# Layer 1's FFN: another order of TensorE's and VectorE's work within a round

## The chip, the cores and the metric

One NeuronCore of a Trainium2 chip runs the whole kernel as one program. The metric is the time of one execution on the device in microseconds (us), as the median of several runs.

## The reference

Two transformer layers on 1024 tokens (4 x 256) of width 512, each an attention and an FFN with a layer norm behind each of the four. The change touches only the last of the four, layer 1's FFN:

```python
result = jnp.einsum('bsi,oi->bso', x, W) + b                  # "base": 512 -> 512
q = jnp.einsum('bsi,ni->bsn', x, Wq).reshape(Bt, S, E, DK)    # E = 8 experts, DK = 32
k = jnp.einsum('bsi,ni->bsn', x, Wk).reshape(Bt, S, E, DK)
scores = jnp.einsum('bsed,bsed->bse', q, k) / math.sqrt(DK)
w = jax.nn.softmax(scores, axis=-1)                           # "gate"
h = jnp.einsum('bsi,eri->bser', x, A)                         # rank R = 16 each
combined = jnp.einsum('bse,bser,eor->bso', w, h, Bm)
x = _layernorm(x + result + combined)                         # the layer norm at the end
```

(The program prints `x + _L1_ffn_ref(x)`; the residual is folded into the rows that are added at the end of a tile.)

## The kernel before

The 1024 tokens are 8 tiles of 128 (`NT` = 8). Class `FFN1` (L2406) gives each engine its own program; each goes through rounds t = 0 to 8 (`rounds`, L2443): rounds 0 and 1 are written out, rounds 2 to 5 are a loop of two iterations with two rounds each, rounds 6, 7 and 8 are written out again. Every operand is kept as a high and a low part, so every product is three matmuls (`matmul3`: lines 106, 107, 108 are its three).

What TensorE does in a round t from 1 to 5, in its order (`round_` in `tensor`, L2730 on): `queries(t)`, 12 matmuls of 320 columns into bank `bq` (q and half of h); `turn_weighted(t - 1)`, one transpose of the weighted rows `wh` of the tile before into `bw`; `keys`, 12 matmuls of 320 columns into `bk` (k and the other half of h); `combined(t - 1)`, 3 matmuls of 512 columns that finish the sum of the tile before in `br`; `turn(t + 1)`, 4 transposes of the next tile's tokens `x` into `bx`; `base(t)`, 12 matmuls of 512 columns into `br`. `queries(t)` first waits for `xT_lo` of tile t, `turn(t + 1)` for `x` of tile t + 1, `turn_weighted` for `wh`, `combined` for `whT_lo`. Round 6 puts `queries(7)` and `keys(7)` after half of `base(6)`; round 7 holds `turn_weighted(6)`, the rest of `base(6)`, `combined(6)` and three quarters of `base(7)`; round 8 the rest.

VectorE in round t (`round_` in `vector`, L2659 on): `begin(t + 1)` writes `x` of the next tile (L2527); in rounds 0 and 1 statistics of later tiles of the norm before; `whT_lo` (L2669); then `gates_and_end` (L2603). That one mixes two chains. The gate of tile t: `gate_product` (L2544, waits for `bk`), `gate_scores` (L2548), `gate_max` (L2553), `gate_scaled_max` (L2557), after ScalarE's exponential `gate_weights` (L2562 to L2570, writes `wh`). The end of tile t - 1: `end_sum` (L2579, waits for `combined`), `end_stats` (L2584), `end_mean` (L2589), `end_var` (L2594), after GpSimd's power `end_out` (L2600, writes `yo`). Between them stands `xlo(t + 1)` (L2532, writes `xT_lo`, waits for ScalarE's `xT_hi`). A step that reads what VectorE has just written waits for it with a semaphore (`after`).

ScalarE in round t: `qs` (L2500), `whT_hi` (L2504), `xT_hi` of tile t + 1 (L2495), the exponential (L2509). GpSimd in round t (`round_` in `gpsimd`, L2475 on): `with_bias(t + 1)` (L2473, writes `xb`; it waits for `end_mean` of tile t - 1), in round 1 alone the power of four later tiles' variances of the norm before (`norm.power(pool, 4, 8)`, L1117), then the power of tile t - 1 (L2484, writes `rs`, for which `end_out` waits):

```python
if has(t + 1, NT):
    with_bias(t + 1, 1 - u)
if isinstance(t, int) and t == 1:
    norm.power(pool, 4, 8)
if has(t - 1, NT):
    ...
    pool.tensor_tensor(rstd[:, :], mean[:, 1:2], m["mh"][:, 0:1], ALU.pow).then_inc(s_rs, 1)
```

All queues run in program order; no planner sets it. SyncE only stores finished tiles.

Of the kernel before, what the change touches and what calls it, by code (L numbers as in the profile page):

```python
# [41 lines left out]
NT = T // P  # L42
KC = HID // P
# [24 lines left out]
def f32(ap):  # L68

    return ap.bitcast(F32)  # L70


def transpose(pe, out, rows, ident):

    return pe.transpose(out.bitcast(F32R), rows, ident)  # L75


def need(eng, sem, value):

    if isinstance(value, int) and value <= 0:  # L80
        return
    eng.wait_ge(sem, value)
# [16 lines left out]
def has(x, n):  # L99

    return not isinstance(x, int) or 0 <= x < n
# [2304 lines left out]
class FFN1:  # L2406
# [4 lines left out]
    def __init__(self, k, io, g, raw, norm):  # L2411
# [118 lines left out]
        def xlo(dve, t, u):  # L2530
            dve.wait_ge(s_xhi, t + 1)
            dve.tensor_tensor(xT[u][1][:, :], bx[:, :], f32(xT[u][0][:, :]), ALU.subtract).then_inc(s_xlo, 1)  # L2532

        def vector(dve, added):

            def after(sem, value):

                dve.wait_ge(sem, value)
                plain(dve, g["tick"])

            def gate_product(t, u):
                dve.wait_ge(s_q, t + 1)
                dve.wait_ge(s_bk, t + 1)
                dve.tensor_tensor(prod[:, :], bk[u][:, 0:E * DK], qs[:, :], ALU.mult).then_inc(s_gate, 1)  # L2544

            def gate_scores(t):
                after(s_gate, NGATE * t + 1)
                dve.tensor_reduce(sc[:, :], prod[:, :].rearrange("p (e d) -> p e d", e=E), AX, ALU.add)\  # L2548
                   .then_inc(s_gate, 1)

            def gate_max(t):
                after(s_gate, NGATE * t + 2)
                dve.tensor_reduce(nm[:, :], sc[:, :], AX, ALU.max, negate=True).then_inc(s_gate, 1)  # L2553

            def gate_scaled_max(t):
                after(s_gate, NGATE * t + 3)
                dve.tensor_scalar(nms[:, :], nm[:, :], inv, None, ALU.mult).then_inc(s_gate, 1)  # L2557

            def gate_weights(t, u):
                dve.wait_ge(s_ex, t + 1)  # L2560
                plain(dve, g["tick"])
                dve.reciprocal(ri[:, :], sm[:, :]).then_inc(s_gate, 1)  # L2562
                after(s_gate, NGATE * t + 5)
                dve.tensor_scalar(gate[:, :], ex[:, :], ri[:, 0:1], None, ALU.mult).then_inc(s_gate, 1)
                after(s_gate, NGATE * t + 6)
                need(dve, s_tw, t)
                for i, bank in enumerate((bq[u], bk[u])):
                    es = slice(i * E // 2, (i + 1) * E // 2)
                    h = bank[:, E * DK:W1H].rearrange("p (e r) -> p e r", e=E // 2)
                    dve.tensor_tensor(wh[:, es, :], h, gate[:, es][:, :, None].to_broadcast([P, E // 2, R]),  # L2570
                                      ALU.mult).then_inc(s_wh, 1)

            def end_tiles(t):
                return (y, st, mv, rs) if not isinstance(t, int) or t < NT - 1 else (x[0], st_last, mv_last, rs_last)

            def end_sum(t, v):
                dve.wait_ge(s_r, t + 1)
                dve.wait_ge(s_xb, t + 1)
                dve.tensor_tensor(end_tiles(t)[0][:, :], br[v][:, :], xb[v][:, :], ALU.add).then_inc(s_end, 1)  # L2579

            def end_stats(t):
                rows, stats, _, _ = end_tiles(t)
                after(s_end, NEND * t + 1)
                dve.bn_stats(stats[:, :], rows[:, :]).then_inc(s_end, 1)  # L2584

            def end_mean(t):
                _, stats, mean, _ = end_tiles(t)
                after(s_end, NEND * t + 2)
                dve.bn_aggr(mean[:, :], stats[:, :]).then_inc(s_end, 1)  # L2589

            def end_var(t):
                var = end_tiles(t)[2][:, 1:2]
                after(s_end, NEND * t + 3)
                dve.tensor_scalar(var, var, EPS, None, ALU.add).then_inc(s_var, 1)  # L2594
# [8 lines left out]
            def gates_and_end(t, u, before):  # L2603

                now, last = has(t, NT), has(t - 1, NT)
                early = isinstance(t, int) and t == NT - 2
                v = 1 - u
                if now:
                    gate_product(t, u)
                if last:  # L2610
                    end_sum(t - 1, v)
                if early:
                    xlo(dve, t + 1, v)
                if now:
                    gate_scores(t)
                if last:
                    end_stats(t - 1)
                if now:
                    gate_max(t)
                if last:  # L2620
                    end_mean(t - 1)
                if now:
                    gate_scaled_max(t)
                if last:
                    end_var(t - 1)
                if has(t + 1, NT) and not early:
                    xlo(dve, t + 1, v)
                if now:
                    gate_weights(t, u)
                if last:  # L2630
                    end_out(t - 1, v, before)
# [53 lines left out]
        def turn(pe, t, u):  # L2685
            pe.wait_ge(s_x, t + 1)
            need(pe, s_xlo, t)
            for c in range(KC):
                i = transpose(pe, bx[:, c * P:(c + 1) * P], x_t[u][:, c * P:(c + 1) * P], ident[:, :])
            i.then_inc(s_tx, 1)  # L2690
# [6 lines left out]
        def tensor(pe):  # L2697

            def queries(t, u):
                pe.wait_ge(s_xlo, t + 1)  # L2700
                need(pe, s_wh, 2 * t - 2)
                wide(pe, bq[u], u, HID, W1H, True).then_inc(s_bq, 1)

            def keys(u):
                wide(pe, bk[u], u, HID + W1H, W1H, True).then_inc(s_bk, 1)

            def turn_weighted(t):
                pe.wait_ge(s_wh, 2 * t + 2)
                need(pe, s_whl, t)
                transpose(pe, bw[:, 0:P], wh_t[:, :, :].rearrange("p e r -> p (e r)"), ident[:, :]).then_inc(s_tw, 1)  # L2710

            def combined_last():
                out, hi, lo = br[1][:, :], whT[0][:, :], whT[1][:, :]
                pe.wait_ge(s_whT, NT)
                pe.matmul(out, hi, bm[0], start=False, stop=False, skip_group_check=True)
                pe.matmul(out, hi, bm[1], start=False, stop=False, skip_group_check=True)
                pe.wait_ge(s_whl, NT)
                pe.matmul(out, lo, bm[0], start=False, stop=True, skip_group_check=True).then_inc(s_r, 1)

            def combined(t, v):  # L2720
                pe.wait_ge(s_whl, t + 1)
                if isinstance(t, int) and t == 0:
                    pe.wait_ge(raw["s_lo"], KC + 1)
                matmul3(pe, br[v][:, :], (whT[0][:, :], whT[1][:, :]), bm, False, True).then_inc(s_r, 1)

            def base(t, u, chunks=range(KC)):
                need(pe, s_end, NEND * (t - 2) + 1)
                wide(pe, br[u], u, 0, HID, False, chunks)

            def round_(t, u, i):  # L2730
                if isinstance(t, int) and t == NT - 1:
                    turn_weighted(t - 1)
                    base(t - 1, 1 - u, range(2, KC))
                    combined(t - 1, 1 - u)
                    base(t, u, range(KC - 1))
                    return
                if isinstance(t, int) and t == NT:
                    turn_weighted(t - 1)
                    base(t - 1, 1, range(KC - 1, KC))
                    combined_last()  # L2740
                    return
                if not (isinstance(t, int) and t == 0):
                    queries(t, u)
                    turn_weighted(t - 1)
                keys(u)
                if has(t - 1, NT):
                    combined(t - 1, 1 - u)
                turn(pe, t + 1, 1 - u)
                if isinstance(t, int) and t == NT - 2:
                    base(t, u, range(2))  # L2750
                    queries(t + 1, 1 - u)
                    keys(1 - u)
                else:
                    base(t, u)

            rounds(pe, round_)

        self.begin, self.xlo, self.turn, self.first = begin, xlo, turn, first
# [77 lines left out]
```

## Time and profile before

| | |
|---|---|
| time, median of 3 runs | 1416.83 us (1416.5 to 1417.45) |
| the profiled execution | 1415.87 us, its span 1414.1 us |
| mean granted TensorE clock | 0.999 |
| TensorE busy | 1400.2 us (99% of the span) |
| VectorE, ScalarE, GpSimd busy | 72%, 63%, 55% |
| stage of layer 1's FFN | from about 1347 us to the end |

Times in the rows are us from the start of the span. A matmul's recorded duration is longer than its step: matmuls are pipelined, so the distance from one start to the next is what one costs.

### The profile page before, as it was taken

What the parts mean: (1) busy time and instruction counts of PE and PEld (TensorE: products, weight loads), DVE (VectorE), ACT (ScalarE), POOL (GpSimd) and SP (SyncE); (2) the same over time, 40 slices, a digit from 0 to 9 for tenths busy, and PEclk for the clock granted to TensorE, in tenths of its full rate; (3) what the DMA queues carried; (4) which work ended last, traced back from release to release, by engine and by line L of the source; (5) the groups of instructions that cost most, each with busy time, mean ns of one, the idle gap of its engine ahead of it and who ended that gap; (6) DMA issues with size and microseconds to landing.
All of it is one profiled execution on the core that took longest, in us unless ns stands there. A gap on an engine that the chain in (4) does not pass through costs nothing.

```text
span 1414.1 us, 30207 instructions
## 1 busy us (share of the span) xinstructions
PE 1400.2 (99%) x8769; PEld 1236.6 (87%) x8769; DVE 1017.3 (72%) x2528; ACT 891.2 (63%) x2445; POOL 774.0 (55%) x828
## 2 busy tenths in 40 slices
PE   9999999999999999999999999999999999999998
PEld 7898889888788878889889889889889889889887
DVE  5999999999968875665665665665665665665776
ACT  5888888888555576555556556556556556556711
POOL 3555555555040467765765765665665665665521
PEclk9999999999999999999999999999999999999999
DMA  5533333322445301111101011001002001000201
GB/s 197 169 95 95 95 95 95 94 66 51 134 135 164 97 31 61 31 31 59 30 30 59 30 30 59 30 30 59 30 30 59 30 30 59 30 30 30 83 16 46
DMA packets 56155, 92.60 MB, mean 65 GB/s; under 512 B 6064, under 2 KB 27312, under 8 KB 56112
## 3 DMA queue, kind: packets, MB, share of 16 engines
q1 hardware_dynamic: 55968, 91.93, 21.3%
q8 instruction: 23, 0.38, 0.1%
q14 instruction: 20, 0.16, 0.0%
q10 hardware_dynamic: 144, 0.13, 0.0%
HBM read 81.82 MB, written 2.10 MB: 59 GB/s over the span
## 4 chain that ended last, share of the span: by engine, by line
PE 94%; DVE 2%; ACT 1%; issue 1%; POOL 1%; DMA 1%; SPq 0%; POOLq 0%; DVEq 0%; ACTq 0%
PE c_bv L106 8%; PE c_bv L108 7%; PE c_bv L107 7%; PE c_bx L106 5%; PE h_bo L944 5%; PE c_bx L108 4%; PE c_bx L107 4%; PE c_by L106 4%; PE c_by L108 4%; PE c_by L107 4%; PE h_bo L1447 3%; PE a_acc L1447 3%; PE h_bt L75 3%; PE h_bs L106 2%; PE c_bt L75 2%; PE h_bs L108 2%
## 5 line engine op out<-in xcount | busy, mean ns | idle before, releaser
L618 POOL TENSOR_TENSOR h_pr<-h_pr,h_rinv 128x512 f32<-128x512 f32 x128 | 133.2, 1041 | 136.7 <-DVE h_rinv L769 134.3
L1778 POOL TENSOR_TENSOR c_qk<-g_y,c_qk 128x512 fp32r<-128x512 f32 x96 | 124.0, 1292 | 147.3 <-ACT c_qk L1890 140.6
L1629 POOL TENSOR_TENSOR b_sw_lo<-b_slots,b_sw_hi 128x512 fp32r<-128x512 f32 (+1 forms) x128 | 148.1, 1157 | 10.2
L1627 POOL CAST b_sw_hi<-b_slots 128x512 fp32r<-128x512 f32 (+1 forms) x128 | 72.6, 567 | 143.6 <-DMA b_slots<-in_w_qk 125.5
L106 PE MATMUL c_bv<-b_wv_hi,g_xT_hi 128*128 128x256 f32 x496 | 138.8, 280 | 0.2 <-DVE g_xT_lo L1183 0.2
L108 PE MATMUL c_bv<-b_wv_hi,g_xT_lo 128*128 128x256 f32 x496 | 138.8, 280 | 0.0
L107 PE MATMUL c_bv<-b_wv_lo,g_xT_hi 128*128 128x256 f32 x496 | 138.7, 280 | 0.0
L1999 DVE TENSOR_TENSOR c_bo<-c_bo,g_wo 128x128 f32<-128x128 f32 x128 | 38.3, 300 | 122.3 <-ACT g_wo L1865 117.6
L1890 ACT ACTIVATE c_qk<-g_y 128x512 fp32r<-128x512 f32 x96 | 60.7, 632 | 96.5 <-DVE g_y L2036 67.1
L671 ACT ACTIVATE h_pr<-h_bs,h_nmax 128x256 f32<-128x256 f32 x256 | 119.3, 480 | 2.5 <-DVE h_nmax L764 2.4
L1855 ACT ACTIVATE c_pr<-c_pr,c_rinv 128x128 f32<-128x128 f32 (+1 forms) x256 | 101.8, 448 | 9.1 <-DVE c_rinv L1989 9.1
L1847 ACT ACTIVATE c_pr<-g_wo,c_nmax 128x128 f32<-128x128 f32 x128 | 51.5, 403 | 84.3 <-DVE c_nmax L1985 84.3
L107 PEld LDWEIGHTS c_bv<-b_wv_lo,g_xT_hi 128*128 128x128 f32 x496 | 93.1, 188 | 4.7
L106 PEld LDWEIGHTS c_bv<-b_wv_hi,g_xT_hi 128*128 128x128 f32 x496 | 93.0, 187 | 4.7 <-DVE g_xT_lo L1183 0.3
L1609 POOL TENSOR_TENSOR b_slots<-b_slots 128x256 f32<-128x256 f32 x128 | 93.8, 755 | 2.5
L108 PEld LDWEIGHTS c_bv<-b_wv_hi,g_xT_lo 128*128 128x128 f32 x496 | 93.1, 188 | 0.0
L2017 DVE TENSOR_TENSOR g_res<-c_bv,g_res 128x512 f32<-128x512 f32 x103 | 71.2, 692 | 27.2 <-PE c_bv L108 27.2
L764 DVE TENSOR_REDUCE h_nmax<-h_bs 128x2 f32<-128x512 f32 x128 | 87.5, 684 | 0.0
L773 DVE TENSOR_TENSOR h_pt_lo<-h_bt,h_pt_hi 128x512 fp32r<-128x512 f32 x128 | 87.2, 681 | 0.2
L1860 ACT ACTIVATE c_pt<-c_bt 128x384 fp32r<-128x384 f32 x128 | 62.9, 491 | 35.3 <-PE c_bt L75 31.5
L1865 ACT ACTIVATE g_wo<-c_bo 128x128 f32<-128x128 f32 x128 | 35.3, 276 | 77.3 <-PE c_bo L2262 77.3
L106 PE MATMUL c_bv<-b_wo_hi,c_oT 128*128 128x512 f32 x200 | 81.4, 407 | 0.0
(480 smaller groups left out, 5140.2 us busy)
## 6 DMA issues: line engine op xcount, KB each, us to landing
f_wi<-in_w_ffn SPq DMA_DIRECT2D x66, 256.0 KB, 2.7
b_slots<-in_w_qk SPq DMA_DIRECT2D x64, 256.0 KB, 3.0
a_w<-in_w_head SPq DMA_DIRECT2D x28, 352.0 KB, 2.9
h_part<-in_w_ffn SPq DMA_DIRECT2D x32, 264.0 KB, 2.7
b_raw_v<-in_w_v SPq DMA_DIRECT2D x16, 512.0 KB, 4.5
b_raw_o<-in_w_o SPq DMA_DIRECT2D x16, 512.0 KB, 4.5
h_o_mix<-h_o_hi SPq DMA_DIRECT2D x62, 128.0 KB, 2.2
b_ffn_w<-in_w_ffn SPq DMA_DIRECT2D x4, 576.0 KB, 5.6
```

Source lines behind the costliest of these rows:

```text
L106: pe.matmul(out, w[0], x[0], start=start, stop=False, skip_group_check=True)
L107: pe.matmul(out, w[0], x[1], start=False, stop=False, skip_group_check=True)
L108: return pe.matmul(out, w[1], x[0], start=False, stop=stop, skip_group_check=True)
L618: pool.tensor_tensor(pr[b][:, :, :], pr[b][:, :, :], rinv[b][:, :][:, :, None].to_broadcast([P, 2, S]), ALU.mult)\
L671: m = act.activation(pr[b][:, i, :], bs[b % 2][:, i * S:(i + 1) * S], ACT.Exp, bias=nmax[b][:, i:i + 1], accum_out=rsum[b][:, i:i + 1])
L764: dve.tensor_reduce(nmax[b][:, :], bs[b % 2][:, :].rearrange("p (a n) -> p a n", a=2), AX, ALU.max, negate=True).then_inc(s_max, 1)
L773: dve.tensor_tensor(pt[b][1][:, :, :], bt[b % 2][:, :].rearrange("p (a n) -> p a n", a=2), f32(pt[b][0][:, :, :]), ALU.subtract).then_inc( ...
L1447: m = pe.matmul(out, a, b, start=start and i == 0, stop=stop and i == len(pairs) - 1, skip_group_check=True)
L1609: pool.tensor_tensor(slot(out), slot(a), slot(b), op).then_inc(self.s_comb, 1)
L1629: pool.tensor_tensor(self.sw[1][:, a:b], self.slots[:, a:b], f32(self.sw[0][:, a:b]), ALU.subtract)\
L1778: pool.tensor_tensor(lo, src, f32(hi), ALU.subtract).then_inc(s_sumlo, 1)
L1855: m = act.activation(x[:, cols], x[:, cols], ACT.Identity, scale=rinv[t % 2][:, i:i + 1])
```

## The change

On TensorE, in rounds 1 to 6, `turn_weighted(t - 1)` moves from between `queries` and `keys` to behind `keys`, directly ahead of `turn(t + 1)`; `combined(t - 1)` moves from behind `keys` to behind the first half (two of four chunks) of `base(t)`; the second half of `base(t)` follows it. In round 6 `combined(5)` stands between the first half of `base(6)` and `queries(7)`. On VectorE, in all rounds but 7 and 8, the four steps of the gate follow one another, then comes `xlo(t + 1)`, and only then the four steps of the end of tile t - 1. ScalarE's, GpSimd's and SyncE's programs stay as they are.

```diff
                 if now:
                     gate_product(t, u)
-                if last:
-                    end_sum(t - 1, v)
                 if early:
                     xlo(dve, t + 1, v)
                 if now:
                     gate_scores(t)
-                if last:
-                    end_stats(t - 1)
-                if now:
                     gate_max(t)
-                if last:
-                    end_mean(t - 1)
-                if now:
                     gate_scaled_max(t)
-                if last:
-                    end_var(t - 1)
                 if has(t + 1, NT) and not early:
                     xlo(dve, t + 1, v)
+                if last:
+                    end_sum(t - 1, v)
+                    end_stats(t - 1)
+                    end_mean(t - 1)
+                    end_var(t - 1)
                 if now:
                     gate_weights(t, u)
...
                 if not (isinstance(t, int) and t == 0):
                     queries(t, u)
-                    turn_weighted(t - 1)
                 keys(u)
                 if has(t - 1, NT):
+                    turn_weighted(t - 1)
+                turn(pe, t + 1, 1 - u)
+                base(t, u, range(2))
+                if has(t - 1, NT):
                     combined(t - 1, 1 - u)
-                turn(pe, t + 1, 1 - u)
                 if isinstance(t, int) and t == NT - 2:
-                    base(t, u, range(2))
                     queries(t + 1, 1 - u)
                     keys(1 - u)
                 else:
-                    base(t, u)
+                    base(t, u, range(2, KC))
```

## Rows read from the trace of the kernel before

**Rows 1.** The page: busy time, share of the span and instructions of TensorE.
```profile
PE 1400.2 (99%) x8769; PEld 1236.6 (87%) x8769; DVE 1017.3 (72%) x2528; ACT 891.2 (63%) x2445; POOL 774.0 (55%) x828
```

**Rows 2.** Windows, the last stretch: five engines' busy us, granted clock, DMA share, GB/s.
```profile
1406.40:1414.10 7.70, 1.63 (x8) 1.02 (x6) 3.49 (x11) 1.09 (x2) 1.29 (x3) 0.80 0.21 72
```

**Rows 3.** Timeline of TensorE: start us, us, engine, line, operation; where queries follow.
```profile
1376.29 0.39 PE L108 MATMUL e_br<-b_ffn_hi,e_xT_lo 128*128 128x512 f32 x1
1376.75 0.41 PE L106 MATMUL e_bq<-b_ffn_hi,e_xT_hi 128*128 128x320 f32 x1
1377.00 0.31 PE L107 MATMUL e_bq<-b_ffn_lo,e_xT_hi 128*128 128x320 f32 x1
...
1398.47 0.41 PE L106 MATMUL e_bq<-b_ffn_hi,e_xT_hi 128*128 128x320 f32 x1
```

**Rows 4.** Timeline of TensorE in round 3: keys, combined, tokens turned, base.
```profile
1371.11 0.31 PE L107 MATMUL e_bk<-b_ffn_lo,e_xT_hi 128*128 128x320 f32 x1
...
1372.72 0.39 PE L106 MATMUL e_br<-b_ffn_hi,e_whT_hi 128*128 128x512 f32 x1
...
1373.41 0.45 PE L75 MATMUL e_bx<-g_ident,e_x_t 128*128 128x128 f32 x4
1373.70 0.47 PE L106 MATMUL e_br<-b_ffn_hi,e_xT_hi 128*128 128x512 f32 x1
1374.01 0.40 PE L107 MATMUL e_br<-b_ffn_lo,e_xT_hi 128*128 128x512 f32 x1
```

**Rows 5.** Timeline of VectorE in round 3.
```profile
1373.62 0.69 DVE L2579 TENSOR_TENSOR e_y<-e_br,e_xb 128x512 f32<-128x512 f32 x1 [0.20 <-PE e_br L108]
...
1375.38 0.18 DVE L2589 BATCH_NORM_AGGREGATE e_mv<-e_st 128x2 f32<-128x6 f32 x1
...
1375.93 0.69 DVE L2532 TENSOR_TENSOR e_xT_lo<-e_bx,e_xT_hi 128x512 fp32r<-128x512 f32 x1
```

**Rows 6.** Timeline of TensorE and ScalarE in round 1.
```profile
1353.75 0.30 PE L106 MATMUL e_bq<-b_ffn_hi,e_xT_hi 128*128 128x320 f32 x1
...
1355.99 0.27 ACT L2504 ACTIVATE e_whT_hi<-e_bw 128x128 fp32r<-128x128 f32 x1
```

**Rows 7.** Timeline of VectorE in round 0: the gate's chain with nothing between its steps.
```profile
1351.49 0.42 DVE L2548 TENSOR_REDUCE e_sc<-e_prod 128x8 f32<-128x256 f32 x1 [0.15 <-DVE e_prod L2544]
...
1352.45 0.68 DVE L2532 TENSOR_TENSOR e_xT_lo<-e_bx,e_xT_hi 128x512 fp32r<-128x512 f32 x1
```

**Rows 8.** Timeline of VectorE in round 8: the end's chain with nothing between its steps.
```profile
1408.07 0.69 DVE L2579 TENSOR_TENSOR e_x<-e_br,e_xb 128x512 f32<-128x512 f32 x1 [0.30 <-PE e_br L2718]
...
1409.74 0.18 DVE L2589 BATCH_NORM_AGGREGATE e_mv<-e_st 128x2 f32<-128x6 f32 x1
```

**Rows 9.** Timeline of GpSimd in rounds 1 and 3.
```profile
1360.37 1.29 POOL L2473 TENSOR_TENSOR e_xb<-e_x,b_ffn_b 128x512 f32<-128x512 f32 x1 [10.37 <-DVE e_mv L2589]
1361.62 1.02 POOL L1117 TENSOR_TENSOR g_rs<-g_mv,g_mh 128x4 f32<-128x4 f32 x1
1362.61 0.55 POOL L2484 TENSOR_TENSOR e_rs<-e_mv,g_mh 128x1 f32<-128x1 f32 x1
...
1375.64 1.28 POOL L2473 TENSOR_TENSOR e_xb<-e_x,b_ffn_b 128x512 f32<-128x512 f32 x1 [5.96 <-DVE e_mv L2589]
```

**Rows 10.** Timeline of VectorE from round 1 into 2, and in round 3.
```profile
1363.19 0.55 DVE L2600 TENSOR_SCALAR e_yo<-e_y,e_mv,e_rs 128x512 f32<-128x512 f32 x1 [1.00 <-POOL e_rs L2484]
1363.73 0.55 DVE L2527 TENSOR_SCALAR e_x<-g_res,g_mv,g_rs 128x512 f32 x1
...
1369.81 0.55 DVE L2600 TENSOR_SCALAR e_yo<-e_y,e_mv,e_rs 128x512 f32<-128x512 f32 x1
1370.27 0.54 DVE L2527 TENSOR_SCALAR e_x<-g_res,g_mv,g_rs 128x512 f32 x1
```

**Rows 11.** Timeline of VectorE and TensorE at the end of round 7.
```profile
1405.94 0.21 DVE L2570 TENSOR_TENSOR e_wh<-e_bk,e_gate 128x64 f32<-128x64 f32 x1
...
1406.37 0.23 PE L75 MATMUL e_bw<-g_ident,e_wh_t 128*128 128x128 f32 x1
```

## The prediction, made before the changed kernel ran

> **What bounds the kernel now.** I read the page's busy times first: TensorE is busy for 1400.2 of 1414.1 us [rows 1], so before the last few microseconds only two things can be worth time: a gap in TensorE's row, or a matmul more or less. The change neither adds nor removes an instruction that computes; it can only open or close gaps in the rounds of layer 1's FFN. Next I read TensorE's timeline start to start. Inside the keys a 320-column matmul costs (1372.72 - 1371.11) / 11 = 0.146 us, inside base a 512-column one (1376.29 - 1374.01) / 10 = 0.228 us [rows 3, 4]. Where queries follow base the distance is 0.46 instead of 0.228, and the second matmul of the queries follows after 0.25 instead of 0.146 [rows 3]: a stall of 0.23 and a restart of 0.10. VectorE's timeline tells why: `xT_lo` begins at 1375.93 and ends at 1376.62, the queries start 0.13 later [rows 3, 5]. It is the last of a chain through gate and end steps that alternate, and the sum `y` at its head had to wait for `combined` [rows 5].
>
> **What the change can give.** I add up TensorE's work from the queries of round 1 (1353.75) to those of tile 7 (1398.47), which is 44.72 us before [rows 3, 6]. New round, without a stall: 24 matmuls of 320 columns, 24 x 0.146 = 3.51; the weighted rows' transpose 0.07 (an estimate: four transposes take 0.29 [rows 4]; it could be up to 0.11, or 0.05 if the array takes it for less); the tokens' turn 0.29 and 0.08 extra for the matmul behind it (0.31 against 0.228) [rows 4]; 15 x 0.228 = 3.42. That is 7.37. Round 6 up to the queries of tile 7 has 9 instead of 15 wide ones: 6.00. Five rounds and this one: 36.85 + 6.00 = 42.85, so 1.87 us less than 44.72. With the restart of tile 7's queries (0.10) the most that can be had is 1.97 us. It is made of the six waits ahead of queries and some 0.04 per round for one pause at a transpose instead of two. The second `base` call adds a wait for a semaphore that was passed long ago; behind it only TensorE's own matmuls are queued, and I take it at nothing (at most 0.05 us a round, a sixth of what goes).
>
> Does `xT_lo` now come in time? Yes. The tokens are turned right behind the keys, so that 15 wide matmuls (3.42 us) instead of 12 stand between their turn and the next queries, and on VectorE nothing of the end stands ahead of `xT_lo` any more: in the times worked out below, `xT_lo` of tile 2 ends at 1360.24 and queries could start at 1361.12.
>
> **What is late next.** The end of tile t - 1 now comes after `xT_lo` on VectorE and after a `combined` that stands 1.7 us (turn and half of base) behind the place it had. What hangs on the end: `end_mean` releases GpSimd's `xb`, behind which GpSimd's power of the same tile is queued; `end_out` waits for the power; `begin` of the tile after next stands behind `end_out` on VectorE; and TensorE's `turn` waits for that `x`, which now is wanted about 0.7 us earlier in the round, with base, `combined` and everything else behind it. Before, this chain had slack: in round 2 `x` was written from 1363.73 [rows 10], and in round 3 from 1370.27 to 1370.81 with the turn at 1373.41 [rows 4, 10].
>
> *Round 1 into round 2.* Turn of the weighted rows at 1353.75 + 3.51 = 1357.26, 0.23 long [rows 11]; ScalarE's `whT_hi` 0.03 later, 0.27 long [rows 6]: 1357.79; `whT_lo` at 1357.82; the gate's product 0.20 behind (0.29 less the overlap of 0.08 that neighbours on VectorE show, 1369.81 to 1370.27 for 0.55 [rows 10]): 1358.02. Product 0.42 plus the pause of 0.15 ahead of a step that needs the one before: scores at 1358.59. From scores to `xT_lo` with nothing between, 0.96 [rows 7]: 1359.55. `end_sum` 0.61 later, 1360.16; `combined` is over by then (1357.26 + 0.07 + 0.37 + 6 x 0.228 = 1359.07, and 2 x 0.228 + 0.39 to its end: 1359.92). From sum to mean in an unmixed chain 1.67 [rows 8]: 1361.83, ended 1362.01. GpSimd starts 0.08 later [rows 5, 9]; `xb` takes 1.25, the four tiles' power, which only this round has, 0.99, and the tile's own power 0.55 [rows 9]: 1364.88. `end_out` 0.03 later, `x` 0.54 after that, 0.55 long [rows 10]: 1366.00, and with the 0.13 that TensorE needed after `xT_lo` the turn can start at 1366.13. TensorE is there at 1353.75 + 7.37 + 3.51 + 0.07 = 1364.70. Stall 1.43, restart 0.10: 1.53 us.
>
> *Rounds 3 to 6.* This now is a ring, once around per round. From `combined`'s first matmul to its end 0.85, to `y` 0.05, sum to mean 1.67 [rows 8], mean 0.18 and 0.08 to GpSimd, 1.25, 0.55 and 0.03 to `end_out` [rows 9, 10], 0.46 to `x` inside the loop [rows 10], 0.55, 0.13, restart 0.10, turn and its pause 0.37, six wide matmuls 1.37. Sum 7.64, against 7.37 of work: 0.27 lost per round, four times, 1.08. (The second path, VectorE's from the turned weighted rows to `y`, comes to the same end within 0.1.) Bounds: nothing lost, if the ring is 0.27 shorter; 7.92, if GpSimd's start takes 0.16 as out of the loop, `x` comes 0.54 after `end_out` and this 0.1 later than the power ends. I take the sum of the rows, 7.64; the two ends stay in the range.
>
> *The tail.* Tile 7's queries: -1.87 + 1.53 + 1.08 = +0.74. They start without a restart: -0.10. `wh` of tile 6 comes behind the end of tile 5 on VectorE and is just about late for its turn: +0.08. In round 7 `whT_lo` and the product stand behind `end_out(5)`, late by the ring; before, `wh` ended at 1406.15 and was turned at 1406.37 [rows 11], 0.22 to spare. I take 0.27 for what goes beyond (bounds 0, and 0.5 if all of the lateness is new). Sum: 0.74 - 0.10 + 0.08 + 0.27 = +1.0 us. The chain behind TensorE's last matmul is the same program and shifts along.
>
> So the profiled execution would go from 1415.87 to 1416.9, and as it lies 0.96 below the median of the runs shown, the median from 1416.83 to 1417.8. About 0.2% (2.8 us) is what can be told from no change here.
>
> **A page against the rows.** Between steps that need each other VectorE pauses for 0.15 us [rows 7], while neighbours that do not overlap by 0.08 [rows 10]: un-mixing the two chains costs some 0.23 per pair. The Trainium skill (VectorE: DVE Perf Modes, The DRAIN you can't avoid) says otherwise: the next operation waits for the pipeline to empty in any case, and the semaphore "costs nothing extra here". By that rule the five pairs of the chain into round 2 would be 1.15 shorter and the ring 0.46, below the work; the time would be 1415.2. The rows contradict it.
>
> **The rivals.**
> - *The gain stands.* `x` is not late because the chain through GpSimd is shorter than I add it up. For it: each hop's 0.03 to 0.13 is read from other neighbours. Against it: 1.4 us in round 2 are too much for such errors. 1416.83 - 1.97 = 1414.9.
> - *Pairs that need each other cost no more than others.* Mechanism as above: stall 1.43 - 1.15 = 0.28 and restart 0.10 in round 2, none later: 1416.83 - 1.97 + 0.38 = 1415.2.
> - *The ring is long.* 7.92: another 1.12: 1418.9. For it: waits inside the loop are for values in registers.
> - *Slower: the clock.* TensorE's granted clock is 0.999 in the mean; only the last stretch, busy for 1.63 of 7.70 us, shows 0.80 [rows 2]. The new idle of 1.43 us in round 2 stands in a stage that never stood still so long. If the clock fell from 2.4 to 1.2 GHz behind it, every microsecond of work there would cost one more; from 1.9 such microseconds on (1.0 is already lost) the kernel is slower by more than can be missed, and one round so costs 7.4: 1425. Against it: TensorE works without a pause on both sides. The Trainium skill (TensorE: Matmul & The Clock Gate, Part 1) has activity open the gate and idleness close it; the rows agree in the last stretch alone.
> - *It does not do what it says*: queries still wait in rounds 2 to 6, 0.33 each, with the late `x` besides: 1419.4.
>
> **Numbers.** Forecast 0.63, the gain stands 0.13, free pairs 0.04, long ring 0.12, clock 0.05, the last 0.03. The forecast's own range is 1416.9 to 1418.7. To leave out no more than 2 in 10 the range goes down to 1415.2 (most of the two gaining cases inside) and up to 1419.4 (long ring inside, clock outside). Even the whole gain is 1.97 us, under 2.8: faster 0.02, and only with a drifted median. Slower: clock 0.05 and a share of the cases at 1419: 0.07. Same: 0.91.
>
> **What would show it.** Ahead of queries in rounds 2 to 7 the distance from base's last matmul is 0.228: the first part is right. A gap of about 1.4 us ahead of the tokens' turn in round 2, released by `x` (L2527), with `end_out` waiting for GpSimd: the second. Gaps of about 0.15 there in rounds 3 to 6 and rounds of 7.6 instead of 7.75 us: the ring. A round 2 of 7.4 us would refute me, as would a granted clock below 1.00 there.

## The result, and the profile after

| | before | changed kernel |
|---|---|---|
| median of 22 runs each | 1416.91 us (1416.2 to 1417.53) | 1419.07 us (1418.32 to 1419.87) |
| ratio, 95% interval | | 1.0016 (1.001 to 1.0021) |
| profiled execution, its span | 1415.87, 1414.1 us | 1419.03, 1417.2 us |
| stage: first queries of tile 0 to the last `end_out`, both starts | 1347.02 to 1410.89: 63.87 us | 1347.45 to 1413.19: 65.74 us |

The kernel is 2.2 us (0.16%) slower; 1417.8 was forecast, with 1415.2 to 1419.4 as the range. The spans of the two profiled executions differ by 3.1 us, of which 0.43 arose before the stage, in code that the change does not touch, and 0.8 behind the start of the last `end_out`, while the last rows are stored. Over the ten kernels of this document, which all do the same there, that last stretch took 3.2 to 4.0 us. The stage itself is 1.87 us longer, and by that number I compare below; it is read from one profile of each kernel. All medians and ratios are of fast runs: one execution each of before, `bias_early_tile7` and `combined_after_quarter` took 2358 to 4764 us, in the slow state, and is left out.

The page of the changed kernel, TensorE's and the other engines' busy time:

```profile
PE 1400.6 (99%) x8769; PEld 1238.2 (87%) x8769; DVE 1021.8 (72%) x2528; ACT 891.7 (63%) x2445; POOL 774.1 (55%) x828
```

The same number of instructions as in [rows 1]; VectorE is busy for 4.5 us more, which is the first hint that some of its instructions last longer (the eight scalings of the gate, L2564, account for 3.1 of it, as seen below). Windows of the stage (five engines' busy us, granted clock, DMA share, GB/s):

```profile
1361.80:1366.60 4.80, 3.56 (x26) 3.34 (x24) 3.21 (x10) 0.66 (x2) 2.80 (x3) 1.00 0.02 3
1366.60:1400.00 33.40, 32.90 (x189) 29.23 (x190) 25.76 (x69) 7.21 (x21) 7.25 (x8) 1.00 0.11 40
```

In round 2 TensorE idles for 1.24 of 4.80 us, and the clock stays at 1.00 there and behind. TensorE's timeline, in round 2, round 3 and round 4:

```profile
1361.37 0.39 PE L108 MATMUL e_br<-b_ffn_hi,e_xT_lo 128*128 128x512 f32 x1
1361.60 0.30 PE L106 MATMUL e_bq<-b_ffn_hi,e_xT_hi 128*128 128x320 f32 x1
...
1365.12 0.22 PE L75 MATMUL e_bw<-g_ident,e_wh_t 128*128 128x128 f32 x1
1366.57 0.54 PE L75 MATMUL e_bx<-g_ident,e_x_t 128*128 128x128 f32 x4 [1.24 <-DVE e_x L2527]
1366.95 0.47 PE L106 MATMUL e_br<-b_ffn_hi,e_xT_hi 128*128 128x512 f32 x1
...
1373.96 0.22 PE L75 MATMUL e_bw<-g_ident,e_wh_t 128*128 128x128 f32 x1
1374.23 0.54 PE L75 MATMUL e_bx<-g_ident,e_x_t 128*128 128x128 f32 x4
...
1381.61 0.22 PE L75 MATMUL e_bw<-g_ident,e_wh_t 128*128 128x128 f32 x1
1382.19 0.54 PE L75 MATMUL e_bx<-g_ident,e_x_t 128*128 128x128 f32 x4 [0.36 <-DVE e_x L2527]
```

Queries now follow base's last matmul after 0.23 us (1361.37 to 1361.60), in this round and in all up to tile 7's; before it was 0.31 to 0.47, 0.46 in [rows 3]. That wait is gone. In its place the tokens' turn (`e_bx`) stands 1.45 us behind the weighted rows' turn in round 2, 0.27 in round 3 and 0.58 in round 4, where 0.06 would do without a wait. It starts at 1366.57, 1374.23, 1382.19, 1389.84 and 1397.50 in rounds 2 to 6, so a round lasts 7.66, 7.96, 7.65 and 7.66 us.

What it waits for is seen on VectorE and GpSimd, round 1 into round 2:

```profile
1360.59 0.68 DVE L2579 TENSOR_TENSOR e_y<-e_br,e_xb 128x512 f32<-128x512 f32 x1
1361.42 0.69 DVE L2584 BATCH_NORM_STATS2 e_st<-e_y 128x6 f32<-128x512 f32 x1
1362.26 0.18 DVE L2589 BATCH_NORM_AGGREGATE e_mv<-e_st 128x2 f32<-128x6 f32 x1
...
1363.05 0.87 DVE L2564 TENSOR_SCALAR e_gate<-e_ex,e_ri 128x8 f32<-128x8 f32 x1
...
1365.42 0.55 DVE L2600 TENSOR_SCALAR e_yo<-e_y,e_mv,e_rs 128x512 f32<-128x512 f32 x1 [1.00 <-POOL e_rs L2484]
1365.97 0.55 DVE L2527 TENSOR_SCALAR e_x<-g_res,g_mv,g_rs 128x512 f32 x1
```
```profile
1362.59 1.30 POOL L2473 TENSOR_TENSOR e_xb<-e_x,b_ffn_b 128x512 f32<-128x512 f32 x1 [12.16 <-DVE e_mv L2589]
1363.85 1.02 POOL L1117 TENSOR_TENSOR g_rs<-g_mv,g_mh 128x4 f32<-128x4 f32 x1
1364.84 0.55 POOL L2484 TENSOR_TENSOR e_rs<-e_mv,g_mh 128x1 f32<-128x1 f32 x1
```

Sum, statistics, mean, then GpSimd's `xb`, the four tiles' power, the tile's power, `end_out`, `x`: hop by hop the chain of the prediction, with `x` at 1365.97 where 1365.45 plus the 0.43 of offset was worked out. GpSimd's three durations are those of [rows 9] within 0.02. What is not of the prediction is the 0.87 us of the gate's scaling (L2564), which had 0.23 to 0.47 before. At the end of the stage it costs time. VectorE in round 6, then TensorE:

```profile
1402.97 0.86 DVE L2564 TENSOR_SCALAR e_gate<-e_ex,e_ri 128x8 f32<-128x8 f32 x1 [0.15 <-DVE e_ri L2562]
...
1404.12 0.21 DVE L2570 TENSOR_TENSOR e_wh<-e_bk,e_gate 128x64 f32<-128x64 f32 x1
```
```profile
1403.38 0.31 PE L108 MATMUL e_bk<-b_ffn_hi,e_xT_lo 128*128 128x320 f32 x1
1404.39 0.28 PE L75 MATMUL e_bw<-g_ident,e_wh_t 128*128 128x128 f32 x1 [0.70 <-DVE e_wh L2570]
```

The turn of tile 6's weighted rows comes 1.01 us behind the last matmul of the keys, of which 0.15 is that matmul's step: 0.86 us of waiting. Between rounds 3 and 4 stands the other thing that the prediction lacks, VectorE's `x` 0.77 us behind `end_out` (0.46 in rounds 3, 5 and 6):

```profile
1380.82 0.55 DVE L2600 TENSOR_SCALAR e_yo<-e_y,e_mv,e_rs 128x512 f32<-128x512 f32 x1
1381.59 0.55 DVE L2527 TENSOR_SCALAR e_x<-g_res,g_mv,g_rs 128x512 f32 x1 [0.22 <-issue]
```

### The profile page after: what moved, and what is told of

The parts are those of the page before. It is cut to its first block, busy times and chain, and to the rows that moved or that the text cites. A ratio compares the mean times of both kernels' runs of the same rounds, so it can differ in the third digit from the quotient of the medians.

```text
span 1417.2 us, 30207 instructions
## 1 busy us (share of the span) xinstructions
PE 1400.6 (99%) x8769; PEld 1238.2 (87%) x8769; DVE 1021.8 (72%) x2528; ACT 891.7 (63%) x2445; POOL 774.1 (55%) x828
## 4 chain that ended last, share of the span: by engine, by line
PE 90%; DVE 3%; POOL 2%; issue 2%; ACT 1%; DMA 1%; SPq 0%; DVEq 0%; POOLq 0%; ACTq 0%
PE c_bv L106 8%; PE c_bv L108 7%; PE c_bv L107 7%; PE h_bo L944 5%; PE c_bx L106 5%; PE c_bx L108 4%; PE c_bx L107 4%; PE c_by L106 4%; PE c_by L108 4%; PE c_by L107 4%; PE h_bo L1447 3%; PE a_acc L1447 3%; PE h_bt L75 3%; PE h_bs L106 2%; PE h_bs L108 2%; PE h_bs L107 2%
```

## The experiments

Eight kernels, each timed beside before, with 5 to 12 runs each. The last column is the stage as in the table above, from one profile of each; before has 63.87, the changed kernel 65.74. The changed kernel was not run again beside them, and the median of before moved by 0.36 us between the sets, so where I compare with the changed kernel, the stage decides and not the medians.

| kernel | median us | ratio to before, 95% interval | stage us |
|---|---|---|---|
| `tensor_order_only` | 1427.65 | 1.0076 (1.0062 to 1.009) | 73.95 |
| `vector_order_only` | 1421.24 | 1.0031 (1.0019 to 1.0044) | 68.19 |
| `norm_power_first` | 1417.76 | 1.0004 (0.9995 to 1.0013) | 64.84 |
| `bias_early` | 1415.76 | 0.9991 (0.9982 to 1.0) | 62.65 |
| `bias_early_tile7` | 1418.15 | 1.0009 (1.0 to 1.0018) | 65.19 |
| `bias_early_norm_first` | 1416.01 | 0.9991 (0.9982 to 1.0) | 62.38 |
| `before_bias_early` | 1417.09 | 0.9998 (0.9989 to 1.0007) | 63.92 |
| `combined_after_quarter` | 1418.81 | 1.0011 (1.0002 to 1.002) | 65.67 |

The first four ran beside a before of 1416.99 us, the others beside one of 1417.27.

**Each order by itself.** `tensor_order_only` is the changed kernel with `gates_and_end` put back:

```diff
                 if now:
                     gate_product(t, u)
+                if last:
+                    end_sum(t - 1, v)
...
                     gate_scores(t)
+                if last:
+                    end_stats(t - 1)
+                if now:
                     gate_max(t)
...
-                if last:
-                    end_sum(t - 1, v)
-                    end_stats(t - 1)
-                    end_mean(t - 1)
-                    end_var(t - 1)
```

> TensorE in the changed order, VectorE in the order of before. Theory (the two orders need each other): the sum of tile t-1 stands ahead of the scores and of xT_lo on VectorE but is now released by a combined that ends some 2 us later in the round, so xT_lo comes about 1.8 us late for the queries in rounds 2 to 7: about +10 us against before (1426.5 to 1427.5), no gap ahead of the turn of x. Rival (TensorE's order is harmless, the loss of the changed kernel comes from VectorE's order alone): 1415 to 1417.

Measured: 1427.65 us, the stage 10.1 us longer than before's. TensorE in round 3 of this kernel and VectorE ahead of it:

```profile
1370.34 0.39 PE L108 MATMUL e_br<-b_ffn_hi,e_xT_lo 128*128 128x512 f32 x1
1372.54 0.41 PE L106 MATMUL e_bq<-b_ffn_hi,e_xT_hi 128*128 128x320 f32 x1 [1.81 <-DVE e_xT_lo L2532]
```
```profile
1367.54 0.41 DVE L2544 TENSOR_TENSOR e_prod<-e_bk,e_qs 128x256 f32<-128x256 f32 x1
1369.40 0.69 DVE L2579 TENSOR_TENSOR e_y<-e_br,e_xb 128x512 f32<-128x512 f32 x1 [1.46 <-PE e_br L108]
...
1371.71 0.69 DVE L2532 TENSOR_TENSOR e_xT_lo<-e_bx,e_xT_hi 128x512 fp32r<-128x512 f32 x1
```

VectorE stands for 1.46 us with the scores and `xT_lo` queued behind a sum whose `combined` has moved back. `vector_order_only` takes the other half, the kernel before with VectorE's new order:

```diff
-                if last:
-                    end_sum(t - 1, v)
...
+                if last:
+                    end_sum(t - 1, v)
+                    end_stats(t - 1)
+                    end_mean(t - 1)
+                    end_var(t - 1)
```

> VectorE in the changed order, TensorE in the order of before. Theory: the gate's weights now come behind the whole end chain, the gate product is still released by the keys, and the turn of the weighted rows stands early (behind the queries): it waits 0.7 us for wh in every round 2 to 7; +4 to +5 us against before (about 1421.5). Rival (VectorE's order by itself removes the wait for xT_lo and costs nothing): 1415, gaps ahead of the queries gone and none at the turn of the weighted rows.

Measured: 1421.24 us, the stage 4.3 us longer; the queries' waits of rounds 2 to 6 are gone, the turn of the weighted rows waits in rounds 2 to 7 instead. TensorE in round 3:

```profile
1372.41 0.31 PE L108 MATMUL e_bq<-b_ffn_hi,e_xT_lo 128*128 128x320 f32 x1
1373.26 0.28 PE L75 MATMUL e_bw<-g_ident,e_wh_t 128*128 128x128 f32 x1 [0.55 <-DVE e_wh L2570]
```

So the halves cost 10.1 and 4.3 us alone and 1.9 together. With the other engines' programs as they are, neither could be kept without the other.

**The chain through GpSimd, one link at a time.** `norm_power_first` moves one step in GpSimd's round 1:

```diff
+                if isinstance(t, int) and t == 1:
+                    norm.power(pool, 4, 8)
                 if has(t + 1, NT):
                     with_bias(t + 1, 1 - u)
-                if isinstance(t, int) and t == 1:
-                    norm.power(pool, 4, 8)
```

> The changed kernel with one GpSimd step moved: in round 1 the power of four tiles of the norm before (1.0 us, its input is ready since about 1357) stands ahead of xb instead of between xb and the power of tile 0. Theory (x of tile 3 is late in round 2 by the chain through GpSimd): the gap ahead of the turn of x in round 2 falls from 1.45 to about 0.45 us, everything else keeps its length, so 1.0 us less than the changed kernel: 1418.1. Rival (the gap in round 2 is the loop's entry or code that arrives late): the gap and the time stay, 1419.1.

Measured: 1417.76 us, the stage 0.90 us shorter than the changed kernel's. The distance between the two turns in round 2 went from 1.45 to 0.48 us, the rounds behind it kept their length (7.67, 7.98, 7.65 from queries to queries):

```profile
1365.03 0.22 PE L75 MATMUL e_bw<-g_ident,e_wh_t 128*128 128x128 f32 x1
1365.51 0.54 PE L75 MATMUL e_bx<-g_ident,e_x_t 128*128 128x128 f32 x4 [0.26 <-DVE e_x L2527]
```

`bias_early` takes `xb` out of the chain: it waits for the sum of tile t - 1, the last step that reads the buffer that it writes, and no longer for that tile's mean.

```diff
-                need(pool, s_end, NEND * (t - 1))
+                need(pool, s_end, NEND * (t - 2) + 1)
```

> The changed kernel with GpSimd's xb(t+1) waiting for the sum of tile t-1, the last reader of that buffer, instead of for its mean: xb runs beside the statistics, so the tile's power no longer queues behind it, and it is over before the gate's scaling runs on VectorE. Theory (ring over end chain, xb, power, x, turn of x; in round 6 the scaling of the gate held up while xb runs): the ring gets about 0.9 us shorter and falls below TensorE's work; gaps at the turn of x in rounds 3 to 6 go, round 2 keeps 0.2 to 0.5, the 0.86 us wait for wh of tile 6 goes: 3.0 to 3.5 us less than the changed kernel, 1415.6 to 1416.0, faster than before by about 1.2. Rival (VectorE's own work between the turned rows and y sets the rounds, 2.9 us from bw to y): rounds stay at 7.65, only the tail gains: about 1418.

Measured: 1415.76 us, the stage 3.09 us shorter than the changed kernel's and 1.22 shorter than before's. The median is 1.23 us below that of before beside it, a difference whose interval (0.9982 to 1.0) just reaches none. GpSimd, VectorE and TensorE of this kernel in round 2:

```profile
1368.87 1.30 POOL L2473 TENSOR_TENSOR e_xb<-e_x,b_ffn_b 128x512 f32<-128x512 f32 x1 [4.67 <-DVE e_y L2579]
1370.35 0.55 POOL L2484 TENSOR_TENSOR e_rs<-e_mv,g_mh 128x1 f32<-128x1 f32 x1 [0.18 <-DVE e_mv L2594]
```
```profile
1370.58 0.23 DVE L2564 TENSOR_SCALAR e_gate<-e_ex,e_ri 128x8 f32<-128x8 f32 x1
...
1371.68 0.54 DVE L2527 TENSOR_SCALAR e_x<-g_res,g_mv,g_rs 128x512 f32 x1
```
```profile
1365.10 0.22 PE L75 MATMUL e_bw<-g_ident,e_wh_t 128*128 128x128 f32 x1
1365.38 0.54 PE L75 MATMUL e_bx<-g_ident,e_x_t 128*128 128x128 f32 x4
```

`xb` is released by the sum instead of the mean and is over before the variance is ready; `x` of the next tile is written by 1372.22, 0.6 us ahead of its turn in round 3; the rounds from queries to queries are 7.42, 7.40 and 7.41 us from round 3 on, TensorE's bare work. In round 2 the turn still stands 0.28 behind the other one, where 0.06 would do. VectorE's own chain, the rival, would have kept the rounds at 7.65.

**Both edits, and both on the kernel before.** Both kernels take the two diffs above, the one on the changed kernel, the other on before.

> The changed kernel with both GpSimd repairs: xb waits for the sum instead of the mean, and the four tiles' power of the norm before stands ahead of xb in round 1. Theory: no gap at any turn of x; what is left of the gap in round 2 with the early xb alone (about 0.2 us with its restart) goes: 1415.5, 1.4 us faster than before. Rival (x of tile 3 is not what round 2 waits for then): same as with the early xb alone, 1415.8.

> The kernel before (both old orders) with the same two GpSimd edits. Theory (before, the chain over GpSimd had slack and only xT_lo was late): no change, 1416.9, gaps ahead of the queries as before; at most 0.3 us from the scaling in rounds 1 and 6 that overlaps xb. Rival (the early xb is worth its 3 us in any order): below 1415.

Measured: `bias_early_norm_first` 1416.01 us where 1415.5 was expected, its stage 62.38: 0.27 us less than with `bias_early` alone, 1.49 less than before's. The wait in round 2 is gone (0.05 from turn to turn), while the medians (1416.01 beside a before of 1417.27, 1415.76 beside 1416.99) do not tell the two apart. `before_bias_early` 1417.09, its stage 63.92 against 63.87, its queries still wait:

```profile
1376.34 0.39 PE L108 MATMUL e_br<-b_ffn_hi,e_xT_lo 128*128 128x512 f32 x1
1376.78 0.41 PE L106 MATMUL e_bq<-b_ffn_hi,e_xT_hi 128*128 128x320 f32 x1
```

So the GpSimd edits are worth 3.4 us of the stage with the changed order and nothing with the old one: they shorten a chain that only the change made late.

**The scaling of the gate.** `bias_early_tile7` lets only the last `xb` start early:

```diff
-                need(pool, s_end, NEND * (t - 1))
+                need(pool, s_end, NEND * (t - 2) + 1 if isinstance(t, int) and t == NT - 1 else NEND * (t - 1))
```

> The changed kernel with the early xb for tile 7 alone (GpSimd's last one, round 6). Theory (VectorE's scaling of the gate is held for as long as GpSimd's xb runs, 0.86 instead of 0.23 us): in round 6 the scaling takes 0.23, wh of tile 6 comes 0.6 us earlier, the wait ahead of its turn falls from 0.86 to about 0.25; nothing else in the stage moves; 0.5 to 0.6 us less than the changed kernel, 1418.5. Rival (the wait is from the order alone, weights behind the whole end chain): wait and time stay, 1419.1.

Measured: 1418.15 us, the stage 0.55 us shorter than the changed kernel's. GpSimd, VectorE and TensorE of this kernel in round 6:

```profile
1401.09 1.29 POOL L2473 TENSOR_TENSOR e_xb<-e_x,b_ffn_b 128x512 f32<-128x512 f32 x1 [5.03 <-DVE e_y L2579]
```
```profile
1402.73 0.23 DVE L2564 TENSOR_SCALAR e_gate<-e_ex,e_ri 128x8 f32<-128x8 f32 x1
```
```profile
1403.15 0.31 PE L108 MATMUL e_bk<-b_ffn_hi,e_xT_lo 128*128 128x320 f32 x1
1403.52 0.28 PE L75 MATMUL e_bw<-g_ident,e_wh_t 128*128 128x128 f32 x1
```

With `xb` over at 1402.38, the scaling takes 0.23 instead of 0.86 us, and the turn stands 0.37 behind the last matmul of the keys instead of 1.01: the wait fell from 0.86 to 0.22. The gap in round 2 (1.46) and the rounds behind it stayed as they were.

**Combined earlier.**

```diff
-                base(t, u, range(2))
+                base(t, u, range(1))
                 if has(t - 1, NT):
                     combined(t - 1, 1 - u)
                 if isinstance(t, int) and t == NT - 2:
+                    base(t, u, range(1, 2))
                     queries(t + 1, 1 - u)
                     keys(1 - u)
                 else:
-                    base(t, u, range(2, KC))
+                    base(t, u, range(1, KC))
```

> The changed kernel with combined behind one chunk of base instead of two, so the sum is released 0.68 us earlier. Theory (two paths of nearly equal length lead to y, over combined and over VectorE's gate chain, 2.9 us from the turned rows; and the ring closes over either): only some 0.1 us per round can be had, 0.2 to 0.5 in all: 1418.7. Rival (combined alone sets y): the ring falls by 0.68 to 7.0, below TensorE's work, rounds 3 to 6 lose nothing, and round 2's gap is unchanged: about 1417.7.

Measured: 1418.81 us, the stage 0.07 us shorter: hardly anything, less than the 0.2 to 0.5 I had named. In this kernel one round is on time and the next late, 7.39 and 8.16 us in turn, 15.55 for two where the changed kernel has 15.61. TensorE's turns in rounds 4 and 5, and VectorE in round 3, where the sum starts 0.61 us behind `xT_lo`, as closely as two such neighbours do:

```profile
1381.71 0.22 PE L75 MATMUL e_bw<-g_ident,e_wh_t 128*128 128x128 f32 x1
1382.49 0.53 PE L75 MATMUL e_bx<-g_ident,e_x_t 128*128 128x128 f32 x4 [0.56 <-DVE e_x L2527]
...
1389.87 0.23 PE L75 MATMUL e_bw<-g_ident,e_wh_t 128*128 128x128 f32 x1
1389.93 0.47 PE L75 MATMUL e_bx<-g_ident,e_x_t 128*128 128x128 f32 x4
```

```profile
1376.65 0.69 DVE L2532 TENSOR_TENSOR e_xT_lo<-e_bx,e_xT_hi 128x512 fp32r<-128x512 f32 x1
1377.26 0.68 DVE L2579 TENSOR_TENSOR e_y<-e_br,e_xb 128x512 f32<-128x512 f32 x1
```

A `combined` that ends 0.68 us earlier finds VectorE still in the gate's chain. In the changed kernel the sum of this round already stood 0.64 behind `xT_lo` (1376.29 to 1376.93), so there was nearly nothing to be had. The rounds take turns because VectorE's chain begins at the turn of the weighted rows, which stands ahead of the tokens' turn: the wait of 0.72 us in round 4 comes behind it and delays that chain only in the round after. Both paths to `y` have to get shorter, or what follows `y`.

## Why the prediction was right, and where its terms were off

The direction and the mechanism held: slower by less than 0.2%, by a chain that the moved end steps made late. The size did not: +1.0 us was forecast and +2.2 measured, and 1419.07 lies above the forecast's own range (1416.9 to 1418.7). It lies inside the stated range only because room had been left there for the long ring, which is not what happened; that part is luck. Term by term, after the 0.43 of offset:

- *The waits ahead of the queries go, at most 1.97 us with TensorE's order.* The waits went; their worth was put too high. A round without a wait takes 7.41 us on TensorE (1354.19 to 1361.60), not 7.37, as the tokens' turn takes 0.32 and not 0.29 there. `bias_early_norm_first`, in which nothing but one wait of 0.22 and a restart of 0.05 is left, is 1.49 us shorter than before, so the most was about 1.76.
- *Round 2, 1.43 and a restart.* Measured 1.45 - 0.06 = 1.39 and 0.06 at the matmul behind it (0.38 against the 0.32 that it has in round 1, where no turn waits). `norm_power_first` shows that the four tiles' power is 0.97 of it, and `bias_early_norm_first`, where no wait is left, that `xb` is the rest.
- *The ring, 7.64 per round.* Measured 7.66, 7.65, 7.66, and once 7.96. That 7.64 comes out so closely is in part two errors that cancel: `end_out` followed the power after 0.13 us inside the loop, not 0.03 (1396.31 to 1396.44), and the turn followed `x` after 0.06, not 0.13 (1397.44 to 1397.50). In the late round `x` came 0.77 us after `end_out` instead of 0.46, with nothing that the profile shows to wait for, between two iterations of the loop. The upper bound had 0.54 for this. The trace of before has the same 0.76 in the same place (1377.56 to 1378.32), but there `x` was written 2.3 us ahead of its turn, where it cost nothing. From queries of tile 1 to those of tile 7 the sum was +0.74; it is 45.82 - 44.72 = +1.10. Against the forecast the loop's edge added 0.3 and the rounds' own work 0.2, while round 2 and the other waits each came out 0.1 smaller.
- *The tail.* This is the term that was mis-sized most. I gave 0.08 to the wait for tile 6's weighted rows and 0.27 to tile 7's; measured are 0.86 and nothing. The prediction moves the scaling of the gate into the time in which GpSimd computes `xb` and has no term for that; there it lasts until `xb` ends. `bias_early_tile7` splits the 0.86: 0.64 is the scaling held back, 0.22 is the order alone, for which 0.08 was too little. The 0.27 for tile 7's turn came in none of the kernels that keep the new order on both engines, not even in `bias_early_tile7`, where tile 6's wait pushes TensorE back by 0.22 only; why it does not come is open. The trace of before held the warning: in round 6 the same instruction lasted 0.47 us, and ended 0.03 behind `xb`.

```profile
1399.82 1.30 POOL L2473 TENSOR_TENSOR e_xb<-e_x,b_ffn_b 128x512 f32<-128x512 f32 x1 [6.88 <-DVE e_mv L2589]
1400.68 0.47 DVE L2564 TENSOR_SCALAR e_gate<-e_ex,e_ri 128x8 f32<-128x8 f32 x1
```

- *Pairs that need each other cost 0.23 more.* Right: statistics 0.83 us after the sum and mean 0.84 after the statistics, 1.67 together as in [rows 8]. What costs is waiting for the step just before, not a semaphore as such: `y` waits for two semaphores that had been passed and starts 0.60 us after an `xT_lo` of 0.68 (1359.99 to 1360.59). By the rule that the prediction took from the Trainium skill (VectorE: DVE Perf Modes, The DRAIN you can't avoid) the time would have been 1415.2. The traces do not bear it out for such pairs; that neighbours overlap fits the section's own remark that a next operation that is not held starts earlier.
- *The clock.* It stayed at 1.00 behind an idle of 1.24 us; that rival is out.
- *The gain stands; the ring is long; it does not do what it says.* None came, although the time is near the long ring's 1418.9: what filled the difference was mostly the tail and one loop edge, not 0.28 per round.

## What to carry to other kernels

A step that is moved behind others on one engine takes along everything that hangs on it on other engines: follow it around, through each queue it passes, until it comes back to the bound engine, and compare that ring with the work of a round. Here the ring of 7.65 us stood against 7.41 of work, and the same reordering lengthened the stage by 1.9 us or shortened it by 1.2, depending on whether GpSimd's 1.3 us add, which `end_out` does not need, stood in the ring. When an instruction is moved in time, its price has to be read again beside what the neighbour engine does then, not taken from its old place.

## What the runs showed of the hardware

GpSimd's add of two 128x512 tiles in SBUF holds back VectorE's scaling of a 128x8 tile in SBUF by a pointer scalar. The stage of the changed kernel has seven such adds; in the six that overlap a scaling, the scaling ended 0.03 to 0.04 us after the add, from 1363.05 to 1363.92 against 1363.89 in round 1, with 0.80 to 0.87 instead of 0.23 us. VectorE's reciprocal in front of it took its usual 0.16 us within the add, and so did the statistics, 0.69 us, in `bias_early`, where they run beside it. VectorE's 128x1 `tensor_scalar` by a constant (L2594) kept its 0.15 us too, at 1371.29 inside the add of 1371.22 to 1372.52. And GpSimd's powers did not hold the scaling. In `bias_early` it took its 0.23 us inside the recorded time of the 128x4 power, and again beside the 128x1 power (1370.58, the power from 1370.35 to 1370.90):

```profile
1362.67 1.01 POOL L1117 TENSOR_TENSOR g_rs<-g_mv,g_mh 128x4 f32<-128x4 f32 x1
1363.04 0.23 DVE L2564 TENSOR_SCALAR e_gate<-e_ex,e_ri 128x8 f32<-128x8 f32 x1
```

The Trainium skill (SBUF — State Buffer, Who interferes with whom) says that a `tensor_scalar` in a two-port mode and a GpSimd instruction exclude each other for the whole instruction, whoever comes first. The trace agrees for the scaling beside the add (0.80 to 0.87 us), but not beside the powers (0.23 us). Which mode the scaling ran in no run here shows.
